# The row that VectorE compares for the one-hot tiles: an int16 row in SBUF, or a float32 row in PSUM

## The reference

```python
msg = x[src] * edge_weight[:, None]; agg = segment_sum(msg, dst)      # layer 0
msg = relu(x[src] + edge_attr);      agg = segment_sum(msg, dst)      # layer 1
msg = cat([x[dst], x[src] - x[dst]]) @ W.T + b; h = segment_sum(msg, dst)   # layer 2, then a batch norm
```

## Time and profile before

| | |
|---|---|
| median of 3 runs | 8059.67 us (8032.0, 8059.67, 8060.22) |
| the profiled execution | 8032.9 us, span 8031.1 us |
| first gather of pass 0, of pass 1 and the end of pass 2's gathers | about 21, 1926 and 5710 us |
| busy | PE 4542.0, DVE 4522.3, ACT 993.3, POOL 5800.2 us |
| hot tiles (line 2137) | 2604 + 1736 + 1736 = 6076, 298 ns each |
| gathers (line 906) | 2960 + 1551 + 1482, of 962 to 966 ns |

### The profile page before, as it was taken

The page is one execution under the profiler, slowest core; times in us unless marked ns, Lnnn a source line. Parts: engine busy times, 40 slices in busy tenths (PEclk is TensorE's granted clock), DMA queues, the critical chain, the costliest instruction groups (busy, mean ns, idle before and its releaser), DMA issues. The chain is left out here.

```text
span 8031.1 us, 133429 instructions
## 1 busy us (share of the span) xinstructions
PE 4542.0 (57%) x26578; PEld 3836.9 (48%) x26579; DVE 4522.3 (56%) x12211; ACT 993.3 (12%) x3180; POOL 5800.2 (72%) x6027
## 2 busy tenths in 40 slices
PE   3566566663466666665366666666613556555555
PEld 2455565553345454444244454454313555555555
DVE  4555555554556555654444554554534666666666
ACT  0000000000000000000000000000201233434333
POOL 7777777776777777777677777777267777777771
PEclk6778878786677778877577887778755666666667
DMA  2211111112322222222211111111444555555553
GB/s 64 44 36 33 35 33 36 34 35 47 69 61 62 61 62 62 61 62 55 44 33 33 33 33 34 32 34 32 132 128 111 129 144 138 146 137 142 143 142 87
DMA packets 678635, 570.23 MB, mean 71 GB/s; under 512 B 443949, under 2 KB 451931, under 8 KB 677808
## 3 DMA queue, kind: packets, MB, share of 16 engines
q1 hardware_dynamic: 430048, 295.34, 13.4%
q0 software_dynamic: 191776, 203.12, 13.0%
q10 hardware_dynamic: 55984, 63.18, 2.3%
HBM read 454.34 MB, written 100.74 MB: 69 GB/s over the span
## 5 line engine op out<-in xcount | busy, mean ns | idle before, releaser
L906 POOL DMA_INDIRECT gat<-x_d,idx x2960 | 2846.6, 962 | 956.0 <-issue 901.3
L906 POOL DMA_INDIRECT gat<-rel_d,idx x1551 | 1498.4, 966 | 633.0 <-issue 472.7
L906 POOL DMA_INDIRECT gat<-in_x,idx x1482 | 1429.6, 965 | 466.2 <-issue 451.6
L1426 PE MATMUL p_all<-oh,gat 128*128 128x256 f32 x1568 | 627.6, 570 | 797.5 <-DMA gat<-x_d,idx 757.4
L1412 PE MATMUL p_all<-oh,msg 128*66 128x128 f32 x3136 | 610.9, 377 | 778.6 <-DVE oh L1869 778.6
L1426 PE MATMUL p_all<-oh,msg 128*128 128x256 f32 x1568 | 597.9, 548 | 759.3 <-DVE oh L1869 401.3
L1412 PEld LDWEIGHTS p_all<-oh,msg 128*66 128x66 f32 x3136 | 551.3, 203 | 821.4 <-DVE msg L1995 803.2
L1426 PEld LDWEIGHTS p_all<-oh,gat 128*128 128x128 f32 x1568 | 426.5, 285 | 941.3 <-DMA gat<-x_d,idx 841.2
L1869 DVE SCALAR_TENSOR_TENSOR oh<-dstf,fine_col,p_a 128x512 f32<-128x512 f32 x1176 | 823.6, 741 | 23.7 <-DVE sum_t L1968 4.7
L1426 PEld LDWEIGHTS p_all<-oh,msg 128*128 128x128 f32 x1568 | 407.4, 272 | 885.4 <-ACT msg L1060 809.9
L1580 PE MATMUL p_b<-oh,msg 128*72 128x128 f32 x3136 | 662.1, 399 | 68.1 <-ACT msg L1169 38.5
(11 more groups left out here) (299 smaller groups left out, 6839.4 us busy)
## 6 DMA issues: line engine op xcount, KB each, us to landing
spare<-x_d SPq DMA_DIRECT2D x5888, 0.2 KB
spare<-x_d ACTq DMA_DIRECT2D x5888, 0.2 KB
he_d<-gat ACTq DMA_DIRECT2D x196, 288.0 KB
ea<-he_d SPq DMA_DIRECT2D x196, 288.0 KB
ea<-in_edge_attr SPq DMA_DIRECT2D x196, 256.0 KB
drow<-dst_d SPq DMA_DIRECT2D x196, 256.0 KB
gat<-x_d,idx POOLq DMA_INDIRECT x2960
spare<-in_x SPq DMA_DIRECT2D x2944, 0.2 KB
```

What stands on the lines that cost most here:

```text
L906: nc.gpsimd.indirect_dma_start(out=gat[:, q, s, :] if width == HROW else got[:, q, s, :], out_offset=None, in_=table, in_offset=bass.Indir ...
L1426: ins = nc.tensor.matmul(p_sum[:, c % 2, 0:2 * W], rows_of(s), oh[:, c % 2, s:s + 2, :].rearrange("p s w -> p (s w)"), start=(s == 0), sto ...
```

## The change

`pick_row` was an int16 tile in SBUF, of which there were two, used in turn (they lay in `drow`). It is now one float32 tile in PSUM, the first 256 columns of bank 1 of `p_a`; the last 128 columns of this bank hold `number_row`, which line 1869 reads. The space in `drow` goes to two more buffers of the ring (16 where there were 14). As there is one row only, it is filled one step later: in the step of the pair's first tiles, just ahead of them, where it was filled at the end of the step before.

```diff
-PICK_HOT = 14
+PICK_HOT = 16
...
-        pick_row = [drow[:, u, 0:2 * P] for u in range(2)]
         hot_of = [oht[:, k * 2 * P:(k + 1) * 2 * P] for k in range(4)]
-        hot_of += [drow[:, u, k * 2 * P:(k + 1) * 2 * P].bitcast(bf16) for u in range(2) for k in range(1, 4)]
+        hot_of += [drow[:, u, k * 2 * P:(k + 1) * 2 * P].bitcast(bf16) for u in range(2) for k in range(4)]
...
+        pick_row = p_a[:, 1, 0:2 * P]
...
-                if t + 2 + PICK_SPAN in PICK[n]:
-                    pair = pairs_before(n) + PICK[n].index(t + 2 + PICK_SPAN)
+                if t + 1 + PICK_SPAN in PICK[n]:
+                    pair = pairs_before(n) + PICK[n].index(t + 1 + PICK_SPAN)
                     dve.wait_ge(s_pick_in, 16 * (pair + 1))
-                    ch(vec.tensor_copy(pick_row[pair % 2], pick_i))
+                    ch(vec.tensor_copy(pick_row, pick_i))
...
-                    vec.tensor_scalar(hot_of[i % PICK_HOT], pick_row[pair % 2], half_col[:, 2 * w:2 * w + 1], None,
+                    vec.tensor_scalar(hot_of[i % PICK_HOT], pick_row, half_col[:, 2 * w:2 * w + 1], None,
                                       ALU.is_equal).then_inc(s_hot, 1)
```

## The result

The changed kernel takes 8011.23 us in the median of 4 runs (8005.49 to 8019.3), against 8055.62 us before; the ratio is 0.9946 with a 95% interval of 0.9934 to 0.9958. Three of the four runs of before lie at 8051.58 to 8060.22 us and one at 8032.0.

A forecast was written before the change was run, and what follows sets the result against it. POOL's gathers were taken to bound the kernel, with slower VectorE tiles covered by its waits. 8032.9 - 37 + 6 = 8002 us, or 8029 on the higher level; the forecast was the middle, 8015, range 7975 to 8062.

The forecast's parts named there:

- What bounds: Passes 0 to 2: POOL goes from gather to gather without waiting for anybody, 944 ns plus a 304 ns gap each.
- The tile: L2137 on VectorE: start to start goes from 0.196 to 0.39 us, 1180 us more over the passes.
- The cover: VectorE's waits of 3.4 to 3.5 us a step absorb 2.4 us more, leaving 1.0; slower tiles priced at nothing.
- What POOL gets back: Gathers in the tile stretches of passes 0 to 2 lose their 11 ns delay: 37 us gained, bounds 0 and 41.
- What L1995 and L2046 take: Passes 0 and 1: these lines' 25 us of gather delay stays and shifts against POOL's beat; 6 us lost.
- the 950 to 957 that were given as a sign of being right: Mean gather (L906) in ns expected in passes 0 and 1 if the forecast holds.
- The sum: Whole kernel: 8032.9 - 37 + 6 = 8002 us against the profiled execution, 31 us off.
- The number: Whole kernel: 8015 us, the middle of levels 8002 and 8029, 0.55% below the median before.
- Collisions that stay: Rival, 16%: tile writing still delays gathers, or L1995 and L2046 take 25 us more; 8032 to 8060 us.
- The higher level made of such collisions too: Rival, 16%: the 27 us between the runs before also go with the tiles, giving 7992 us.
- VectorE as the bound: Rival, 10%: above 0.51 us a tile VectorE falls behind and POOL waits at L906; 8300 us at 0.55 us.
- The reason: Tile stretches: L1869's reading of PSUM costs a gather nothing, so the new tile's won't either, and all 37 us go.

The follow-up runs named there:

- row_i16_psum: The changed kernel with its row as int16 in PSUM in place of float32 (ring of 15): 7992.82 us, ratio 0.9952 to the kernel before.
- psum_quarter_more: The changed kernel with every fourth tile made a second time, into a tile nobody reads: 8022.15 us, beside 8011.85 for the changed kernel.
- i16_weights: row_i16_psum with the edge weights that L1995 multiplies by also copied to PSUM, 16 groups at a time: 7989.9 us, ratio 0.9921 to the kernel before.

## Why the prediction was right, step by step

- **What bounds.** Right: POOL's gathers, with no wait for anybody inside the passes, before and after. With the row in PSUM, doubling VectorE's spare time (row_i16_psum) leaves the ratio as it was, and taking nearly all of it (psum_quarter_more) costs 10 us.
- **The tile.** Forecast 472 ns and 0.39 us from start to start; measured 477 ns and 0.392. L1869, with its column operand and its row in the same bank, was the row to go by.
- **The cover.** Forecast 1.0 us a step left of VectorE's waits; measured 213.8 / 159 = 1.34, 232.5 / 167 = 1.39 and 237.7 / 168 = 1.41. I had left out that VectorE gets something back too: the int16 tile had a mean of 297 to 300 ns over a median of 280, the new one has 476 to 477 over 477. 18 to 20 ns on 12.25 tiles are 0.2 us a step, over half of the difference.
- **What POOL gets back.** Forecast 37 us, and this term was hit. By the mean over an undisturbed gather of the same execution pass 2 went from 955 - 944 = 11 ns to 947 - 946 = 1 ns, 12.6 us on 1260 gathers, a third of the forecast as it should be. Counted in the traces over all three tile stretches: before, 992 gathers begin while a tile runs, and together they lose 37.4 us over undisturbed ones (37.7 in the second profile); after, 1943 do, as VectorE is at its tiles twice as long, and they lose 2.0 us (0.9 in the second profile).
- **What L1995 and L2046 take.** Forecast: the 25 us that passes 0 and 1 lose beyond the tiles become 31. This term is not borne out. Measured after: (957 - 946) x 1198 + (964 - 946) x 1257 = 13 + 23 = 36 us, nearly all that is left there over an undisturbed gather. But the gathers that begin under these two lines lose 28.4 us in the first profile of before and 32.0 in the second, and 33.9 and 32.8 in the two of the changed kernel: a loss of 6 us does not stand out from one execution to the next. The reason given for it does not show either: L2046 meets the start of a gather in 101 of its 167 steps before and in 103 of 168 after, so it fell anywhere in the beat already. Nor does pass 1, with 964 ns, lie within the 950 to 957 that were given as a sign of being right. i16_weights takes one of L1995's two readings out of SBUF and gives pass 0's 12 ns back; so that part was L1995's.
- **The sum.** Forecast 31 us. By the excess over an undisturbed gather it is 10 x 1260 in pass 2, (18 - 11) x 1198 in pass 0 and (24 - 18) x 1257 in pass 1, 12.6 + 8.4 + 7.5 = 28.5 us; counted gather by gather in the second profile of each kernel it is 34 us. The runs give 8027.56 - 7996.24 = 31.3 us on the chip with the quicker gather (with the 14-tile ring) and 8051.39 - 8011.85 = 39.5 us on the one with the slower; what makes these 8 us is open. The two profiled executions, 8032.9 and 8019.3, differ by 13.6 us only; gathers 2 ns longer in the second make up 12 us of what is missing.
- **The number.** That 8015 lies 4 us from 8011.23 is in part luck. It was the middle of 8002 and 8029, one for each level, and not a time that the forecast expected. The profile of the changed kernel has the longer gather, 946 ns; if that marks the slower level, the forecast for it was 8029, 18 us too many, as the runs gained more than 31 us there. The direction and the rough size of the change come from the mechanism, the last few us from having said the middle.
- **The rivals.** Collisions that stay: no, those with the tiles are gone. The higher level made of such collisions too: open in part. Before lies at 8027.56 and 8051.39 us on the two chips, 24 us apart, the changed kernel at 7996.24 (14-tile ring) and 8011.85, 16 us apart; 12 us go with the longer undisturbed gather, and the 8 us that went with the change may have been collisions. Before was not profiled at that level. VectorE as the bound: a real limit, not reached.
- **The reason.** I took it that a row in PSUM frees the gathers, as L1869's rows show. The float32 row in SBUF took half of the gain without PSUM, by letting VectorE wait in POOL's place. That it is nevertheless the row's place is shown by int16 in PSUM against int16 in SBUF, 945 beside 955 ns with the same width, and by twice the tiles from SBUF, 963.

The Trainium skill, "SBUF — State Buffer" (Who interferes with whom), has the order of issue decide who is blocked. By the starts in the traces this does not come out: a gather that starts 10 ns ahead of a float32 copy loses 0.18 us, and the copy loses nothing. It could still hold if the gather takes what it needs some time after its start, which no run shows. The same section has the loser blocked until the other instruction ends. For a gather that loses to a copy the table above agrees. For a tile that loses to a gather it does not: among the float32 tiles into `drow` the longest lost 581 - 342 = 239 ns beside a gather of 944, and copies that begin 40 to 500 ns into a gather lose nothing.

## What to carry to other kernels

Where POOL's gathers are the bound and another engine has time to spare, look at what runs when a POOL instruction begins, and compare its mean in stretches with and without it: 11 ns on 955, in each of three passes, were worth 0.4 to 0.5%. Move a row that many small instructions read to a place where reading it disturbs nobody, even if each instruction gets slower; first work out from the slower engine's waits up to where that is free. A profiled execution can lie on another level than the runs it is compared with, so subtract the undisturbed price of its own execution; and profile each kernel twice before reading a few us out of a difference.

## What the runs showed of the hardware

- A gather and a VectorE instruction that goes over 256 numbers from SBUF to SBUF (a tile from int16 in 0.196 us from start to start, a tile from float32 in 0.26 us, a float32 copy in 0.20 us) exclude each other in parts of the gather; so do a gather and L1995, which reads two float32 tiles in SBUF. Tiles made from a row in PSUM, every 0.26 us (int16) or 0.392 us (float32), left the gathers within 1 ns of undisturbed.
- Two repeating chains can lock into one beat (1.24 us of tiles on POOL's 1.25; gathers every 1.44 us on copies), and which one waits differs: float32 tiles from SBUF cost a gather of pass 2 947 - 943 = 4 ns, float32 copies of the same width 968 - 944 = 24 ns.
- A tile of 256 numbers takes 342 ns from an int16 row in PSUM and from a float32 row in SBUF, 477 ns from a float32 row in PSUM, and 279 ns from an int16 row in SBUF.
- The gather that nothing disturbs took 943 to 944 ns in eight profiles and 946 in five, which is 12 us of this kernel; whether the chip makes the difference is not settled.
